# First attention in units of two slots: scores on two pairs of banks, maxima between them on one

## The reference

```python
qkv = jnp.einsum('bse,ehd->bshd', x, w_qkv)          # 16 heads of 64
logits = jnp.einsum('bqhd,bkhd->bhqk', q, k) / jnp.sqrt(64)
logits = jnp.where(tril, logits, neg)                # causal
probs = jax.nn.softmax(logits, axis=-1)
out = jnp.einsum('bhqk,bkhd->bqhd', probs, v)
```

## Time and profile before

| | us |
|---|---|
| timed runs: lowest, median, highest of 3 | 2619.49, 2623.24, 2625.3 |
| span of the profiled execution | 2619.6 |
| busy in the span: TensorE | 2144.8 |
| busy: DVE | 1558.0 |
| busy: ACT | 1272.3 |
| busy: POOL | 869.7 |

### The profile page before, as it was taken

How to read it: one execution, slowest core, us unless ns; L and a number is a source line. 1 busy time by engine, 2 the same in 40 slices (tenths; PEclk the granted TensorE clock), 3 DMA queues, 4 the chain that set the end, 5 groups by cost and what they waited for, 6 DMA issues and landing times.

```text
span 2619.6 us, 39958 instructions
## 1 busy us (share of the span) xinstructions
PE 2144.8 (82%) x14785; PEld 874.9 (33%) x14789; DVE 1558.0 (59%) x2754; ACT 1272.3 (49%) x2281; POOL 869.7 (33%) x938
## 2 busy tenths in 40 slices
PE   3989999899777788999868778899977687767776
PEld 2434444444312133544312123444422232121122
DVE  3444446456677736555676745655576777786731
ACT  1433333343357853343347864344326465657873
POOL 0656664454410024554511103454443100001203
PEclk9999999999989998999979989999988898899998
DMA  3000010010110010000210000000021100200000
GB/s 82 15 13 24 24 48 13 12 40 25 49 41 17 1 31 13 13 24 29 69 41 21 13 4 28 13 24 29 17 64 39 49 1 17 81 17 3 7 1 8
DMA packets 81200, 69.14 MB, mean 26 GB/s; under 512 B 46672, under 2 KB 62800, under 8 KB 80496
## 3 DMA queue, kind: packets, MB, share of 16 engines
q1 hardware_dynamic: 81008, 66.60, 9.1%
HBM read 57.58 MB, written 8.98 MB: 25 GB/s over the span
## 4 chain that ended last, share of the span: by engine, by line
PE 61%; DVE 21%; ACT 8%; issue 6%; SPq 3%; DMA 1%; POOL 0%; ACTq 0%; POOLq 0%; DVEq 0%
PE banks L898 59%; DVE pmax L2380 5%; ACT ring L1788 3%; DVE part_max L1978 3%; ACT room L1595 1%; SPq L687 1%; ACT p_sum L1788 1%; PE banks L1037 1%; DVE room L2130 1%; DVE h L1948 1%; DVE tmp L1872 1%; DVE stats L1936 1%; DVE room L1872 1%; PE banks L1387 1%; DVE oT L1999 1%
## 5 line engine op out<-in xcount | busy, mean ns | idle before, releaser
L2380 DVE TENSOR_REDUCE pmax<-banks 128x2 f32<-128x1024 f32 x512 | 610.2, 1221 | 191.7 <-PE banks L898 188.2
L898 PE MATMUL banks<-ring,v 128*9 128x512 f32 (+4 forms) x2816 | 557.7, 574 | 0.0
L1978 DVE TENSOR_REDUCE part_max<-banks 128x2 f32<-128x1024 f32 (+3 forms) x384 | 365.4, 957 | 310.0 <-PE banks L898 307.3
L898 PE MATMUL banks<-qT,kT 64*128 64x512 f32 (+4 forms) x2048 | 463.3, 516 | 78.8 <-DVE pmax L2380 36.7
L837 POOL TENSOR_TENSOR p_sum<-p_sum,ring 128x512 f32<-128x512 f32 (+3 forms) x320 | 305.7, 955 | 639.9 <-PE banks L898 417.0
L1788 ACT ACTIVATE ring<-banks 128x512 f32<-128x512 f32 x768 | 416.4, 597 | 127.4 <-PE banks L898 124.7
L1554 ACT ACTIVATE ring<-banks 128x1024 f32<-128x1024 f32 (+3 forms) x320 | 245.5, 767 | 446.4 <-PE banks L898 445.4
L839 POOL TENSOR_TENSOR p_sum<-p_sum,ring 128x512 f32<-128x512 f32 (+3 forms) x320 | 307.8, 962 | 25.1
L898 PE MATMUL banks<-oT 64*128 64x512 bf16 x1024 | 187.4, 401 | 93.3 <-ACT ring L1788 40.3
L870 POOL TENSOR_TENSOR room<-room 128x512 f32<-128x512 f32 x32 | 40.6, 1268 | 662.7 <-ACT room L1595 662.7
L898 PEld LDWEIGHTS banks<-qT,kT 64*128 64x128 f32 (+1 forms) x2048 | 145.3, 167 | 302.0 <-issue 103.4
(11 more groups left out here) (277 smaller groups left out, 2585.2 us busy)
## 6 DMA issues: line engine op xcount, KB each, us to landing
inv_bc<-softmax_inverses SPq DMA_DIRECT2D x64, 256.0 KB, 3.9
w_qk<-in_L_attn_w_qkv SPq DMA_DIRECT2D x64, 64.0 KB, 2.0
low<-in_L_ffn_attention_mask SPq DMA_DIRECT2D x4, 1024.0 KB, 5.8
stage<-rope_constants SPq DMA_DIRECT2D x4, 1024.0 KB, 4.9
x_b<-in_L_attn_x SPq DMA_DIRECT2D x4, 512.0 KB, 4.7
w_v<-in_L_attn_w_qkv SPq DMA_DIRECT2D x32, 64.0 KB, 2.0
stage<-in_L_ffn_w SPq DMA_DIRECT2D x8, 256.0 KB, 6.1
out<-x_b SPq DMA_DIRECT2D x16, 128.0 KB, 1.8
```

What stands on the lines that cost most here:

```text
L898: return pe.matmul(dst, lhsT, rhs, start=start, stop=stop)
L1978: dve.reduce_max(part_max[:, :, t, c], banks[MAX_PAIR[m]][:, :, 0:w], AX).then_inc(sem("row_max"), 1)
L2380: dve.reduce_max(pmax1[:, :, g, t, c], banks[(0, 3)[USE1["max", m, b] % 2]][:, :, :], AX).then_inc(sem("row_max1"), 1)
```

## The change

A pair is now six **units** of two slots each (`double`). In unit i TensorE issues up to three maxima with the two score items 2i + 2 and 2i + 3 between them, a side step, the two value items 2i and 2i + 1, and then what is named for the unit: own maxima in unit 0 with the row of the second half and the projection of queries, keys in unit 1, values in unit 2, three maxima of the next pair in each of units 3, 4 and 5, the row of the first half in unit 4, and a second side step at the unit's end.

Scores alternate between banks1 and banks0, and a score item waits for the exponential two before it. All maxima go to banks3, and each waits for the reduction of the one before it. Maxima and score items have a new order within a pair, the ring has four places, and two tiles give up their room (o_s lies in hn, gelu in mask_rows). The last pairs of batches 1 to 3 keep the order by slots.

```diff
+MAX_TILES = [(1, 0), (0, 0), (3, 0), (2, 0), (4, 1), (4, 0), (6, 1), (5, 1), (5, 0), (6, 0), (7, 0), (7, 1)]
+MAX_ITEMS = [(t, c, min(HALF, (t + 1) * P - c * HALF)) for t, c in MAX_TILES]
+EXP_ITEMS = [(c, j, max(0, j * P - c * HALF)) for c, order in enumerate([(0, 3, 1, 2), (0, 1, 2, 3, 4, 7, 5, 6)]) for j in order]
...
-NEXT_MAX_AT = {5: (0, 1), 6: (2,), 7: (3,), 8: (4, 5), 9: (6,), 10: (7, 8), 11: (9,)}
-OWN_MAX_AT = {0: (10,), 1: (11,)}
...
-MAX_PAIR = (0, 3, 0, 3, 0, 3, 0, 0, 0, 3, 0, 3)
-MAX_BEFORE = (None, None, 0, 1, 2, 3, 4, 6, 7, None, 8, 9)
-ROW_BANK = (6, 0)
...
-RING = 3
+PROJECT_IN = {0: 0, 1: 1}
+VALUES_IN = 2
+ROWS0_IN = 4
+NEXT_MAX_IN = {3: (0, 1, 2), 4: (3, 4, 5), 5: (6, 7, 8)}
+OWN_MAX = (9, 10, 11)
...
+ROW_BANK = (6, 7)
...
+FIRST_PAIRS = [0] + [NP * a for a in range(2, B)]
+LEAD_PAIRS = [NP * (a + 1) - 1 for a in range(1, B)]
...
+def max_pair(n, m):
+
+    if n in FIRST_PAIRS and m < FIRST_MAX:
+        return 0 if m % 2 == 0 else 3
+    return 0 if n in LEAD_PAIRS and m == 10 else 3
...
+def st_pair(n, m):
+
+    return 1 if m % 2 == 0 or n in LEAD_PAIRS else 0
...
+RING = 4
...
                 t, c, w = MAX_ITEMS[m]
...
-                if MAX_BEFORE[m] is not None:
-                    pe.wait_ge(sem("row_max"), NI * n + MAX_BEFORE[m] + 1)
-                elif m == 0 and n:
-                    pe.wait_ge(sem("mrow_evac"), 2 * n)
-                elif m == 1:
+                elif m == 0:
                     pe.wait_ge(sem("v_evac"), 2 * n + 2)
-                elif m == 9:
+                elif m == 6:
                     pe.wait_ge(sem("mrow_evac"), 2 * n + 1)
+                elif max_pair(n, m) == 0:
+                    pe.wait_ge(sem("expd"), NI * n)
+                else:
+                    pe.wait_ge(sem("row_max"), NI * n + m)
...
                 c, j, lo = EXP_ITEMS[m]
...
-                if n or m:
+                elif n in LEAD_PAIRS and m:
                     pe.wait_ge(sem("expd"), NI * n + m)
+                else:
+                    pe.wait_ge(sem("expd"), NI * n + m - 1)
...
+            def double(n, i, steps):
+                a, p = divmod(n, NP)
+                maxima = [(n, k) for k in OWN_MAX] if i == 0 else [(n + 1, k) for k in NEXT_MAX_IN.get(i, ())]
+                if i + 1 < DOUBLES:
+                    scores = [(n, 2 * i + 2), (n, 2 * i + 3)]
+                else:
+                    scores = [(n + 1, 0), (n + 1, 1)][:1 if n + 1 in LEAD_PAIRS else 2]
+                for r in range(3):
+                    if r < len(maxima):
+                        max_item(*maxima[r])
+                    if r < len(scores):
+                        st_item(*scores[r])
+                for step in SLOT_STEPS[a][p * NI + 2 * i]:
+                    side_step(steps, step)
+                pv_item(n, 2 * i)
+                pv_item(n, 2 * i + 1)
+                if i == 0:
+                    max_to_row(n, 1)
+                if i in PROJECT_IN:
+                    if p == NP - 1 and PROJECT_IN[i] == 0:
+                        read_out(pe, ("lna1", a + 1))
+                    project(n + 1, PROJECT_IN[i])
+                if i == VALUES_IN:
+                    project_v(n + 1)
+                if i == ROWS0_IN:
+                    max_to_row(n + 1, 0)
+                for step in SLOT_STEPS[a][p * NI + 2 * i + 1]:
+                    side_step(steps, step)
```

More of the change, by code:

```diff
@@ L1003, in pv_item @@
                 for s in range(2):
-                    last = mm(bank[4][half[s], lo:], v0[q][:, j, half[s]], src[:, s, 0:HALF - lo], start=j == 0, stop=j == 4 * c + 3)
+                    last = mm(bank[4][half[s], lo:], v0[q][:, j, half[s]], src[:, s, 0:HALF - lo], start=j == 0, stop=m in (3, NI - 1))
                 last.then_inc(sem("pv"), 1)
@@ L1478, in _ @@
                 first_pair(0, k)
-            st_item(0, 0)
+            for m in range(2):
+                st_item(0, m)
             for a in range(B):
@@ L1482, in _ @@
                 for p in range(NP):
-                    pair(NP * a + p, p + 1 < NP or a == 0, steps, p == NP - 1 and a > 0)
+                    pair(NP * a + p, steps)
                 if a:
@@ L1494, in _ @@
                     if a + 1 < B:
-                        st_item(NP * (a + 1), 0)
+                        for m in range(2):
+                            st_item(NP * (a + 1), m)
             ctx_last(B - 2)
@@ new lines, in lead_pair, with pair @@
+            def lead_pair(n, steps):
+                a, p = divmod(n, NP)
+                for m in range(1, NI + 1):
+                    if m < NI:
+                        exp_item(n, m)
+                    if m == LEAD_ROWS1_AT + 1:
+                        max_rows(n, 1)
+                    for step in SLOT_STEPS[a][p * NI + m - 1]:
+                        side_step(steps, step)
+                    for k in B_LEAD.get(m - 1, ()):
+                        step1(a - 1, k)
+            def pair(n, steps):
+                if n in FIRST_PAIRS:
+                    exp_item(n, 0)
+                    exp_item(n, 1)
+                if n in LEAD_PAIRS:
+                    lead_pair(n, steps)
+                else:
+                    for i in range(DOUBLES):
+                        double(n, i, steps)
@@ L1834, in _ @@
                 for p in range(NP):
-                    pair(NP * a + p, p + 1 < NP or a == 0, steps, p == NP - 1 and a > 0)
-                for step in SLOT_STEPS[a][NSLOT - 1]:
-                    side_step(steps, step)
+                    pair(NP * a + p, steps)
                 if a:
-                    for k in B_LEAD[NI - 1]:
-                        step1(a - 1, k)
                     sums_out(NP * (a + 1) - 1)
@@ L2459, in pair @@
                             final_max(n, 1)
[L2460 to L2464 removed]
                     if m == 4:
                         contexts(n, 0)
[L2467 removed]
+                    if m == 5:
                         invert(n - 1)
@@ L2472, in pair @@
                         side_step(steps, step)
-                    if lead:
-                        for k in B_LEAD.get(m, ()):
-                            step1(a - 1, k)
+                    for k in B_LEAD.get(m, ()):
+                        step1(a - 1, k)
+            def pair(n, steps):
+                if n in LEAD_PAIRS:
+                    lead_pair(n, steps)
+                else:
+                    for i in range(DOUBLES):
+                        double(n, i, steps)
             def straight(steps):
```

160 lines of the change are left out of this document (87 added, 73 removed).

## The result

The changed kernel takes **2695.45 us** (median, 2694.89 to 2696.71); the kernel before, run beside it on the same chip, takes 2621.36. That is 1.0287 times as long, with a 95% interval of 1.0269 to 1.0305. The profiled execution spans 2693.9 us where the one of before spans 2619.6: 74.3 us more.

A forecast was written before the change was run, and what follows sets the result against it. First attention was taken as bound by TensorE's in-order instruction stream. Eight pairs without side work (+23) and 21 with it (+71) made +94 us, added to the timed median of 2623.24: 2717 us, own range 2680 to 2745, 58%.

The forecast's parts named there:

- Waits between maxima: First attention, maxima on one pair of banks: each waits for DVE's reduce of the one before; a loss of 2.7 us per pair.
- Places (a) to (e): Five waits where projections, row products and maxima share banks or need DVE's reduce; 2.35 us per pair where no side work stands.
- The old gaps: TensorE's 1.12 us of gaps in a pair without side work; said to go with two pairs of score banks, or be replaced.
- Value items in twos: Two value items together save a switch and some fixed part: 0.8 to 1.5 us per pair of heads, 1.1 taken.
- The bare pair: Pair of heads without side work, batch 0, 34.20 us before; forecast 2.8 us longer, eight such pairs +23.
- The side pairs: The 21 pairs in units carrying side steps, seven in each of three batches; forecast 3.4 us longer each, together +71.
- the long waits behind DVE's side steps: Long DVE side steps hold a maximum on the only pair of banks: +1.2 us per side pair, bounded by -1.6 and +3.2.
- POOL's casts of the keys: Wanted as the next pair's first maximum waits for ACT's copy of the value projection; costed at nothing beside that wait.
- The sum: All pairs of first attention together: +94 us on the profiled span of 2619.6 us, giving 2717 us.
- That side work fills the waits: Rival, 15%: the 21 pairs with side work lose nothing, their old gaps of 3 to 7 us holding the new waits; 2646.
- That the round trip is hidden: Rival, 8%: a 512-column maximum comes back within 0.93 us, so the 2.7 us between maxima vanish; 2602 us.
- The falling clock: Rival, 15%: first attention's granted clock falls to 0.93, 7% more of some 1390 us at 1.2 GHz costs 42; 2760.

## Why the prediction was right, and where it was off

The direction and the mechanism held: 2695 measured, 2717 forecast, in the forecast's own range of 2680 to 2745. Step by step:

- *Waits between maxima, 2.7 us per pair:* right. From start to start, the seven round trips that the forecast priced last 1.84, 1.81, 0.96, 1.60, 0.95, 1.59 and 1.28 us; it had worked out 1.80, 1.80, 0.94, 1.59, 0.94, 1.59 and 1.26. Less the covers that it took, that is 2.8 us. The view of waits shows only 2.06 of it (0.53, 0.76, 0.17, 0.17, 0.43), because it counts idle time from the end of the product before: where nothing waits, the next product starts ahead of that end (masks of 0.29 us at 319.96, the next product at 320.07).
- *Places (a) to (e), 2.35 us:* measured 0.32, 0.78, 0.18, 0.78 and 0.18, together 2.24. Moving two of these steps removed both waits of 0.78 in the bare pair, so they were what the text said.
- *The old gaps, 1.12 us:* gone, as said.
- *Value items in twos, 1.1 us:* **this is the mis-sized term.** The run that puts them apart, in the order with rotation, prices them at 2.0 us of busy time per pair, above the forecast's own upper bound of 1.5. Two of them together save the 0.15 that it allowed (1.87 us against twice 1.01) and the switch of 0.09, which makes 1.4 in six units; the other 0.6 is not separated.
- *The bare pair:* 2.8 forecast, 2.07 measured. With 2.0 in the place of 1.1 the same sum gives 2.8 + 2.24 - 1.12 - 2.0 = 1.9.
- *The side pairs, 3.4 us each:* in the six of batch 2 3.2 (299.7 against 280.3), in all eighteen of batches 1 to 3 that lie between two such projections 2.96. In the six of batch 2 the waits for part_max grew by 3.0 a pair, those for row and values by 0.9, and TensorE is busy 0.9 less. Of the 3.0, some 1.5 are the long waits behind DVE's side steps, for which the forecast took 1.2; the other 1.5, by the view of waits, are the short ones, for which the forecast took the full 2.7. POOL's casts of the keys, costed at nothing, cost 1.5 us in the six pairs.
- *The sum, +94 on the span:* +74. First attention has some 71 of it. Of the 23 us that it falls short, about 7 are bare pairs and 8 the eighteen side pairs; the last 8 lie in the openings of the first pairs and in the pairs 14, 22 and 30 with the pair by slots behind each, and no run separates them. The other 3.5 us are in second attention and behind it, which the forecast took to be unchanged.
- *Rivals:* that side work fills the waits falls with 3.2 us a side pair. That the round trip is hidden falls with the 1.8 us between starts; what it would have given, 2602 us, is near what the runs with a short round trip gave, 2595.84 and 2616.91. The falling clock is a small part: first attention of batch 1 went from 0.97 to 0.95 and the second attention behind it from 0.95 to 0.93, while batch 0 rose from 0.96 to 0.98. Worked out as in the prediction's rival, 4% more of 341 and of 282 us at 1.2 GHz cost about 6 and 4 us, and 4% less of 296 us gives back 5 (an estimate, since the clock is shown to two digits); no run separated it. The bare pair stays at 1.00, as said.

What stays open: how much of the time that a short round trip gives back comes by way of the clock, and why the side pairs of batch 1 give the gain of the values in twos back as waits for part_max, while those of batches 2 and 3 keep it. DVE's side steps may lie differently there; no run moved them.

## What to carry to other kernels

Before an operation is given banks of its own, work out its round trip from the trace (start of the product to start of the next one on the same bank) and subtract what stands between; every kind of product that shares an in-order engine needs this, and rotating all kinds together over the same banks covers what one kind alone cannot. Grouping products of one tile shape is worth measuring by itself, since its gain (2.0 us of 33 here) can hide inside a change that loses. In a trace, take the price of a round trip from starts: the idle times between products come out too small. And when one engine's stream is put in a new order, recheck the engines that had room: POOL, with the same 23 us of work, cost a bare pair of the changed kernel nothing and the first kernel with rotation 3.7 us in one wait.

## What the runs showed of the hardware that was not expected

**A wait costs more than its gap.** Three runs have the same stream of products in the bare pair, all at a granted clock of 1.00: with 10 waits TensorE is busy 31.94 us (the changed kernel), with 5 it is 31.54 (short round trip, full load), with 4 it is 31.41 (short round trip). That is some 0.08 us of busy time per wait on top of its gap. The waits of the short round trips differ in length too, so the share of each wait is an estimate. In part it is the counting told above, by which a gap begins only at the end of the product before.

**One long wait brought half clock, many short ones did not.** In the kernel with rotation, the view by stretch around the wait of 3.69 us (the clock is the third number from the end):

```profile
311.00:324.00 13.00, 13.00 (x140) 6.40 (x136) 7.51 (x10) 4.22 (x6) 11.81 (x11) 1.00 0.23 57
324.40:328.00 3.60, 0.10 (x2) 0.00 (x0) 1.65 (x2) 0.34 (x1) 3.38 (x4) 1.00 0.00 0
328.20:331.50 3.30, 3.30 (x18) 2.04 (x20) 1.23 (x1) 0.81 (x1) 0.94 (x2) 0.50 0.02 5
331.60:333.80 2.20, 1.88 (x22) 0.86 (x19) 1.42 (x2) 0.60 (x1) 0.45 (x1) 1.00 0.00 0
```

The granted clock reads 1.00 through the wait and 0.50, which is 1.2 GHz, for the products right behind it; the pair is busy 32.59 us where the one without the wait is busy 31.47. So the wait cost 1.1 us beyond its own length. The same wait of 3.7 us stands in four other pairs ahead of 370 us, and half clock follows each of them, in two a product later; in the first bare pair it is 1.58 us long, and the clock stays at 1.00. The bare pair of the changed kernel, with ten gaps of at most 0.78 us and 4.30 in all, stays at 1.00. The Trainium skill (TensorE: Matmul & The Clock Gate, A second HAM failure mode) tells of short pauses between groups that make the clock swing; no bare pair here that lacks the long wait shows that, whether the pauses are ten of this size or, with the banks given the other way round, 7.6 us in all.
